# Second-layer values: four fp32 products per turn replaced by twelve split products per two turns

## The chip, the cores and the metric

One core of one Trainium2 chip runs the kernel. The metric is the device time of one execution in microseconds (us), lower is better. Engines: PE is TensorE (matmuls into PSUM), DVE is VectorE, ACT is ScalarE, POOL is GpSimd, SP issues DMAs. PSUM has eight banks of 128 x 512 fp32, PB0 to PB7.

## The reference, cut to what matters

Two layers over x of 16 x 64 rows of 512 (1024 rows), all in fp32, each an attention and a feed-forward part with residual additions. The change lies in the second layer's attention (16 query heads, 4 key heads of 96, keys and values from context and latents together: 128 positions per batch element) and in the feed-forward part behind it:

```python
x = x + L0_attention(layernorm(x), ctx)          # 32 heads of 128
x = x + L0_ffn(layernorm(x))                     # top-2 of 4 low-rank experts
# L1 attention: per batch element b, key head kv, query head h
hidden = concatenate([ctx, y], axis=1)           # y = layernorm(x)
attn = softmax(q @ k.T / sqrt(96))               # 64 queries x 128 positions
out = attn @ v                                   # "values", 96 wide
x = x + out @ Wo.T
# L1 ffn: a dense product with an effective weight
x = x + layernorm(x) @ (W + sum_e w_e A_e B_e).T + bias
```

## The kernel before, in words

Products that must keep fp32 accuracy are made in one of two ways. Plain fp32 operands: one matmul, which the trace shows as two records. Or split operands: each operand is kept as a high half of type fp32r and a low half (value less high half), and `thrice` (line 1159) makes three fp32r matmuls, high x high, high x low, low x high, into the same bank. The high half is made by an ACT copy, the low half by a DVE or POOL subtraction.

`plan()` writes one list of steps by hand, and every engine walks the same list and issues, for each step, only its own part. So the order of the list is the order of each engine's queue. `stage` and `tile` give a step a PSUM bank; `opened` is the wait until the bank's last reader is through, `read` the wait until this tile has been read, `done` the wait until PE has filled it.

The second layer's attention works in 32 turns s of four batch elements and two query heads of a key head (key head j = s // 8, quarter qd, head pair pr = s % 2). Two successive turns, 2t and 2t+1, give one pair t, and from it come two output tiles n = 2t and 2t+1. The loop over `it` (line 332, it = 1 to 32) runs a pipeline. One iteration holds, for PE in this order: `c1(it-2)` (four transposes of the probabilities into bank 3, PT), `b1(it-1)` (scores into bank 2), sometimes `v1` or `k1`, until it = 28 a quarter of a query projection `q1` (nine split products), `e1(it-5)` (the output product of one tile, nine split products), `d1(it-2)` (the values of one turn: four fp32 matmuls of 128 columns, eight records, line 1352, into bank 4 or 5), and for it = 29 to 32 `weff` (four matmuls, line 1374, for the effective dense weight).

Around them stand in the same list:
- DVE: row maximum of `b1` (line 1109); `low1(it-3)`, three subtractions of 256 elements that give the low halves of a turn's values (line 1132); `norm1` (reciprocal, line 1117, and multiplication, 1119); the residual addition of `e1` (line 945); for it = 29 to 32 `stats` (966, 968) and `weff`, which adds the product to `w1T` (1149); at it = 32 `rstd`, twelve small operations one after the other (979 to 990).
- ACT: `c1` is the move of the transposed probabilities out of bank 3 (`pTb`); `b1` four exponentials and four read-outs of their sums (913); `d1` three moves of 256 elements which make the high halves of the values `Oh`; for it = 29 to 31 `weff_split`, which waits for DVE's `weff` addition.
- POOL: low halves of weights.

Behind the loop (lines 371 to 404, "the tail") stand `c1(31)`, `weff_split(3)`, `low1(30)`, `e1(28)`, two normalisations `xn`, `d1(31)`, `low1(31)`, `e1(29)`, four transposed tiles `xT(3, 0..3)` with `e1(30)` between the second and the third, `e1(31)`, the statistics and `rstd` of the upper rows, the dense products 0 to 2, `xT` 4 and 5, dense 3, `xT` 6 and 7, dense 4 to 7. Each `e1` adds its result into 128 rows of x, and the second half of the rows can be normalised only when `e1(31)` has been added.

`PACK` (line 12) says how heads of 96 rows are laid into tiles of 128: six pieces of 96, 32, 64, 64, 96 and 32 rows.

Of the kernel before, what the change touches and what calls it, by code (L numbers as in the profile page):

```python
# [62 lines left out]
def plan():  # L63
# [268 lines left out]
    for it in range(1, N1 + 1):  # L332
        if 0 <= it - 2:
            stage("c1", it - 2, bank=3)
        stage("b1", it - 1, bank=2)
        if 0 <= it - 3:
            step("low1", it - 3)
        step("norm1", it - 1)
        for i in v1_plan.get(it, ()):
            v1(1, i)  # L340
# [8 lines left out]
        if 0 <= it - 2:  # L349
            stage("d1", it - 2, bank=4 + it % 2)  # L350
# [27 lines left out]
    stage("d1", N1 - 1, bank=5)  # L378
    step("low1", N1 - 1)
# [39 lines left out]
def program(nc, a, out):  # L419
# [18 lines left out]
    with ExitStack() as ctx:  # L438
# [46 lines left out]
        V1 = [sb(f"V1{r}", [128, 4, 1024]) for r in range(2)]  # L485
# [24 lines left out]
        PS, PT, PA = PB[2], PB[3], PB[4:6]  # L510
# [186 lines left out]
        def gpsimd_program(e):  # L697
            pool = Lane(e)
            for kind, *k in steps:
# [51 lines left out]
                elif kind == "b0":  # L751
# [26 lines left out]
        def scalar_program(e):  # L778
# [161 lines left out]
        def vector_program(e):  # L940
# [6 lines left out]
            for kind, *k in steps:  # L947
# [163 lines left out]
                elif kind == "norm1":  # L1111
# [7 lines left out]
                    e.tensor_tensor(E3, E3, rr.unsqueeze(2).broadcast_to([128, 4, 128]), ALU.mult).then_inc(s_nrm1)  # L1119
                elif kind == "low1":  # L1120
                    s, = k
                    pr, e2, os = s % 2, s % 2, (s // 2) % 2
                    n = 0
                    for m in range(3):
                        for r0, rows, h, d0 in PACK[m]:
                            if h // 2 == pr:
                                n += 1
                                src = PA[e2][d0:d0 + rows, :].rearrange("p (b n t) -> p n b t", b=4, n=2)[:, h % 2]
                                dh, dl = (O[r0:r0 + rows, os, 256 * m:256 * m + 256].rearrange("p (b t) -> p b t", b=4)
                                          for O in (Ohp, Olp))  # L1130
                                dve.wait_ge(s_ohi1, 3 * s + 3)
                                last = e.tensor_tensor(dl, src, dh.bitcast(f32), ALU.subtract)
                    last.then_inc(free[4 + e2])
# [22 lines left out]
        def tensor_program(e):  # L1156
# [14 lines left out]
            for kind, *k in steps:  # L1171
                if kind in ("k0", "q0", "v0", "e0", "sum0", "xT", "k1", "v1", "b1", "c1", "d1", "e1", "weff",
                            "dense", "mgT", "delta"):
                    b = bank_of(kind, *k)
# [168 lines left out]
                elif kind == "d1":  # L1343
                    s, = k
                    j, qd, pr = s // 8, s % 8 // 2, s % 2
                    e2 = s % 2
                    pe.wait_ge(*read("c1", s))
                    for bb in range(4):
                        bt = 4 * qd + bb
                        pe.wait_ge(*read("v1", 0, bt // 2))  # L1350
                        pe.wait_ge(*read("v1", 1, bt // 2))
                        last = e.matmul(PA[e2][0:96, bb * 128:(bb + 1) * 128],  # L1352
                                        V1[bt % 2][:, j, 128 * (bt // 2):128 * (bt // 2) + 96],
# [105 lines left out]
```

## Time and profile before

| | |
|---|---|
| median of 3 runs | 854.36 us (853.88 to 854.86) |
| profiled execution | 854.5 us |
| span of its profile | 852.7 us |
| PE busy | 839.6 us, 98% of the span |
| DVE / ACT / POOL busy | 490.3 / 353.0 / 310.7 us |

The span runs from the first to the last instruction; what the execution's own time has over it (1.8 us) lies around them. A matmul's recorded duration is longer than its share of the stream, because matmuls are pipelined: the pace is the distance between two starts. Layer one ends near 500 us, the 32 turns run from about 599 to 813 us, the tail from there to the end.

### The profile page before, as it was taken

The page shows a single profiled execution, that of the slowest core. Times are in us where ns is not written, and L with a number is a line of the kernel's source. Part 1 is how long each engine was busy: PE and PEld are TensorE (multiplying, and loading weights), DVE is VectorE, ACT ScalarE, POOL GpSimd, SP SyncE. Part 2 cuts the span into 40 slices and gives each one's busy share as a digit, 9 for nine tenths or more (in the row PEclk, how much of TensorE's full clock was granted, in tenths as well). Part 3 has the DMA queues.
Part 4 walks back from the last instruction along what each step waited for, and adds up shares of the span by engine and source line. Part 5 has one row for each costly group of instructions (what it writes and reads, how often), then busy time and mean ns, then how long its engine had stood idle before and what let it go on. Part 6 is the DMA issues. An engine that isn't in the chain of part 4 may idle for free.

```text
span 852.7 us, 12369 instructions
## 1 busy us (share of the span) xinstructions
PE 839.6 (98%) x4758; PEld 700.2 (82%) x4758; DVE 490.3 (57%) x869; ACT 353.0 (41%) x827; POOL 310.7 (36%) x239
## 2 busy tenths in 40 slices
PE   6999999999999999999999999999999999999998
PEld 5878888888888888888877788888988888888776
DVE  6856655655555655555566536465344445455783
ACT  6443123123123123123123242667776766676642
POOL 4777534634534634534536330112010210211222
PEclk9999999999999999999999999999999999999999
DMA  8112211311211311311211122101010110310002
GB/s 302 50 64 75 86 38 41 109 38 38 87 38 39 111 38 38 87 38 40 85 38 52 46 78 81 26 26 50 13 38 13 54 47 1 107 43 1 1 1 100
DMA packets 24891, 48.15 MB, mean 56 GB/s; under 512 B 3584, under 2 KB 4736, under 8 KB 24704
## 3 DMA queue, kind: packets, MB, share of 16 engines
q1 hardware_dynamic: 24400, 47.22, 18.2%
q8 instruction: 38, 0.62, 0.3%
q14 instruction: 21, 0.17, 0.1%
q10 hardware_dynamic: 432, 0.14, 0.1%
HBM read 45.12 MB, written 2.23 MB: 56 GB/s over the span
## 4 chain that ended last, share of the span: by engine, by line
PE 93%; DVE 2%; POOL 2%; ACT 1%; DMA 1%; issue 1%; SPq 0%; POOLq 0%; DVEq 0%
PE PB L1161 22%; PE PB L1163 22%; PE PB L1162 22%; PE PB L1320 8%; PE PB L1251 4%; PE PB L1335 3%; PE PB L1225 3%; PE PB L1352 3%; PE PB L1168 3%; PE PB L1235 1%; PE PB L1272 1%; DMA xs<-in_x 1%; PE PB L1374 1%; POOL qb L730 1%; ACT Eb L809 1%
## 5 line engine op out<-in xcount | busy, mean ns | idle before, releaser
L945 DVE TENSOR_TENSOR xs<-xs,PB 128x512 f32<-128x512 f32 x112 | 76.8, 686 | 120.3 <-PE PB L1163 113.1
L730 POOL TENSOR_TENSOR qb<-qb,arena 128x512 f32<-128x512 f32 x64 | 83.7, 1308 | 151.3 <-DVE arena L1023 151.3
L781 ACT ACTIVATE Oh<-PB 128x512 fp32r<-128x512 f32 (+2 forms) x160 | 69.2, 467 | 82.7 <-PE PB L1352 44.9
L1161 PE MATMUL PB<-WOh,Oh 128*128 128x512 f32 x248 | 96.6, 390 | 0.0
L1163 PE MATMUL PB<-WOh,Ol 128*128 128x512 f32 x248 | 96.5, 389 | 0.0
L1162 PE MATMUL PB<-WOl,Oh 128*128 128x512 f32 x248 | 96.5, 389 | 0.0
L1020 DVE TENSOR_TENSOR qb<-PB,ropeq 128x512 f32<-128x512 f32 x64 | 44.2, 691 | 69.4 <-PE PB L1163 68.3
L707 POOL TENSOR_TENSOR WQl<-stage,WQh 128x512 fp32r<-128x512 f32 x38 | 49.0, 1292 | 91.4 <-ACT WQh L781 90.1
L1161 PE MATMUL PB<-xTh,WQh 128*128 128x512 f32 x192 | 76.5, 399 | 0.0
L1163 PE MATMUL PB<-xTh,WQl 128*128 128x512 f32 x192 | 74.8, 390 | 0.0
L1162 PE MATMUL PB<-xTl,WQh 128*128 128x512 f32 x192 | 74.7, 389 | 0.0
L781 ACT ACTIVATE WOh<-stage 128x512 fp32r<-128x512 f32 (+1 forms) x32 | 19.4, 619 | 132.3 <-PE PB L1163 132.3
L707 POOL TENSOR_TENSOR WOl<-stage,WOh 128x512 fp32r<-128x512 f32 (+1 forms) x32 | 40.4, 1276 | 89.4 <-ACT WOh L781 63.5
L781 ACT ACTIVATE arena<-PB 128x256 f32<-128x256 f32 (+3 forms) x56 | 26.4, 473 | 80.9 <-PE PB L1163 80.5
L1046 DVE TENSOR_TENSOR Ol<-PB,Oh 128x512 fp32r<-128x512 f32 x64 | 39.7, 683 | 33.7 <-ACT Oh L781 33.6
L1163 PEld LDWEIGHTS PB<-WOh,Ol 128*128 128x128 f32 x248 | 46.5, 188 | 9.7
L1161 PEld LDWEIGHTS PB<-WOh,Oh 128*128 128x128 f32 x248 | 46.6, 188 | 9.7
L1162 PEld LDWEIGHTS PB<-WOl,Oh 128*128 128x128 f32 x248 | 46.6, 188 | 9.6
L1109 DVE TENSOR_REDUCE sm<-PB 128x4 f32<-128x512 f32 x32 | 22.1, 691 | 52.3 <-PE PB L1335 52.3
L781 ACT ACTIVATE WQh<-stage 128x512 fp32r<-128x512 f32 x38 | 23.7, 630 | 64.6 <-PE PB L1163 63.7
L913 ACT ACTIVATE Eb<-PB,sm 128x128 f32<-128x128 f32 x128 | 45.0, 365 | 6.8 <-DVE sm L1109 6.5
L1161 PEld LDWEIGHTS PB<-xTh,WQh 128*128 128x128 f32 x192 | 36.0, 188 | 12.8 <-issue 5.8
(212 smaller groups left out, 2080.5 us busy)
## 6 DMA issues: line engine op xcount, KB each, us to landing
stage<-in_wq SPq DMA_DIRECT2D x44, 256.0 KB, 2.9
stage<-in_wo SPq DMA_DIRECT2D x44, 256.0 KB, 2.6
arena<-recs SPq DMA_DIRECT2D x32, 256.0 KB, 3.9
stage<-in_wk SPq DMA_DIRECT2D x13, 256.0 KB, 2.6
arena<-in_ctxT SPq DMA_DIRECT2D x8, 256.0 KB, 4.4
stage<-in_wv SPq DMA_DIRECT2D x8, 256.0 KB, 3.8
xs<-in_x SPq DMA_DIRECT2D x8, 256.0 KB, 5.7
out<-xs SPq DMA_DIRECT2D x8, 256.0 KB, 2.0
```

The source lines that it names most:

```text
L707: e.tensor_tensor(lo, staged[:, n % 4, 0:cols], hi.bitcast(f32), ALU.subtract).then_inc(s_wlo)
L730: e.tensor_tensor(dst, dst, tmp, ALU.add).then_inc(s_radd)
L781: return e.activation(dst, src, ACT.Copy)
L913: last = e.activation(Eb[:, e2, cols], PS[:, cols], ACT.Exp, bias=mx[:, bb:bb + 1], accum_out=rs[:, bb:bb + 1])
L945: e.tensor_tensor(xs[:, i, :], xs[:, i, :], PB[b][:, :], ALU.add).then_inc(free[b])
L1020: e.tensor_tensor(dst, src, table[:, 0:1, :].broadcast_to([128, 8, 64]), ALU.mult)
L1046: e.tensor_tensor(dl, src, dh.bitcast(f32), ALU.subtract).then_inc(free[bank_of("d0", u, h, w)])
L1161: e.matmul(dst, Ah, Bh, start=(k == 0), stop=False)
L1162: e.matmul(dst, Ah, Bl, start=False, stop=False)
L1163: return e.matmul(dst, Al, Bh, start=False, stop=(k == n - 1))
L1251: last = e.matmul(PB[b][:, 256 * c:256 * c + 256], V[rows, i, c0:c0 + 128], E0[u % 2][rows, 512 * h + 256 * c:512 * h + 256 * c + 256], st ...
L1320: last = e.matmul(PB[b][:, :], W[:, m, r], H[:, c, cols], start=(n % 12 == 0), stop=(n % 12 == 11))
```

## The change

- `d1` is done once for two turns: `d1(t)`, at odd `it`, makes for each of four batch elements three fp32r matmuls of 256 columns (128 of either turn; `pTh[:, :, cols]` is two stretches of 128), twelve in all; elements 0 and 1 go to bank 4, 2 and 3 to bank 5. Output tile n needs only the bank n % 2.
- The probabilities are split: ACT's move writes the high half `pTh` (it lies over `pTb`), and a new DVE step `p_low` writes `pTl`; bank 3 comes free with `p_low`.
- The values' weights are split by POOL, one new step `v1_split` of two operations (128 x 384 elements) per pair, a pair ahead.
- ACT's high halves of the values are a step of their own, `o_move(t, bank)`, with six moves of 128 elements; DVE's `low1(t, bank, part)` is twice three subtractions of 128 elements.
- In the tail the step for `e1(30)` stands behind dense 0, and `e1(31)` behind dense 1; only dense 2 is left between `e1(31)` and `xT` 4.
- The scratch that the program reserves for DMA descriptors is made smaller (1024).

The core of it:

```diff
+        t, h = (it - 4) // 2, it % 2
+        if t >= 0 and h == 0:
+            step("o_move", t, h)
         if 0 <= it - 2:
             stage("c1", it - 2, bank=3)
+        if t >= 0 and h == 1:
+            step("o_move", t, h)
+        if 0 <= it - 2 and h == 1:
+            step("p_low", it - 2)
         stage("b1", it - 1, bank=2)
-        if 0 <= it - 3:
-            step("low1", it - 3)
+        if t >= 0:
+            step("low1", t, h, 0)
+        if t >= 0 and h == 1:
+            step("low1", t, h, 1)
+        if 0 <= it - 2 and h == 0:
+            step("p_low", it - 2)
         step("norm1", it - 1)
+        if t >= 0 and h == 0:
+            step("low1", t, h, 1)
+        if h:
+            step("v1_split", it // 2)
...
-        if 0 <= it - 2:
-            stage("d1", it - 2, bank=4 + it % 2)
+        if it % 2 and it >= 3:
+            d1(it // 2 - 1)
...
     stage("c1", N1 - 1, bank=3)
+    t = N1 // 2 - 1
+    step("o_move", t - 1, 1)
     step("weff_split", 3)
-    step("low1", N1 - 2)
+    step("p_low", N1 - 1)
+    low1(t - 1, 1)
     stage("e1", 28)
     for i in range(2):
         step("xn", 3, i)
-    stage("d1", N1 - 1, bank=5)
-    step("low1", N1 - 1)
+    d1(t)
+    step("o_move", t, 0)
+    low1(t, 0)
     step("stats", 3, 4)
...
         if i == 1:
-            stage("e1", 30)
-            step("stats", 3, 6)
+            step("o_move", t, 1)
+            low1(t, 1)
     for i in LO:
         step("add_bias", i)
+    stage("dense", 0)
+    stage("e1", 30)
+    step("stats", 3, 6)
+    stage("dense", 1)
     stage("e1", 31)
     step("stats", 3, 7)
     step("rstd", 3, 4)
-    for i in range(3):
-        stage("dense", i)
+    stage("dense", 2)
     normed(3, HI, [None, lambda: stage("dense", 3)])
...
-                elif kind == "d1":
-                    s, = k
-                    pr, e2, os = s % 2, s % 2, (s // 2) % 2
-                    act.wait_ge(*done("d1", s))
-                    if s >= 4:
-                        act.wait_ge(*done("e1", s // 2 * 2 - 3))
+                    act.wait_ge(*done(*(("d1", s // 2 - 1, 1) if s >= 2 else ("delta", 4 * s + 3))))
+                    move(pTh[:, s % 2, :], PT[:, :]).then_inc(s_phi)
+                elif kind == "o_move":
+                    t, bank = k
+                    act.wait_ge(*done("d1", t, bank))
+                    if t >= 2:
+                        act.wait_ge(*done("e1", 2 * t - 4 + bank))
                     for m in range(3):
                         for r0, n, h, d0 in PACK[m]:
-                            if h // 2 == pr:
-                                src = PA[e2][d0:d0 + n, :].rearrange("p (b n t) -> p n b t", b=4, n=2)[:, h % 2]
-                                dh = Ohp[r0:r0 + n, os, 256 * m:256 * m + 256].rearrange("p (b t) -> p b t", b=4)
-                                move(dh, src).then_inc(s_ohi1)
+                            col = 256 * m + 128 * bank
+                            dh = Ohp[r0:r0 + n, t % 2, col:col + 128].rearrange("p (b t) -> p b t", b=2)
+                            move(dh, PA[bank][d0:d0 + n, h]).then_inc(s_ohi1)
...
+                elif kind == "p_low":
+                    s, = k
+                    dve.wait_ge(s_phi, s + 1)
+                    e.tensor_tensor(pTl[:, s % 2, :], PT[:, :], pTh[:, s % 2, :].bitcast(f32), ALU.subtract).then_inc(free[3])
                 elif kind == "low1":
+                    t, bank, part = k
+                    dve.wait_ge(s_ohi1, 12 * t + 6 * bank + 6)
...
                 elif kind == "d1":
+                    t, = k
+                    pe.wait_ge(s_vlo, t + 1)
+                    pe.wait_ge(*read("c1", 2 * t))
+                    pe.wait_ge(*read("c1", 2 * t + 1))
                     for bb in range(4):
+                        b = bank_of("d1", t, bb // 2)
+                        pe.wait_ge(*opened("d1", t, bb // 2))
+                        cols = slice(128 * bb, 128 * bb + 128)
+                        dst = PB[b][0:96, 256 * (bb % 2):256 * (bb % 2) + 256].rearrange("p (r t) -> p r t", r=2)
+                        last = thrice(dst, 0, 1, V1h[:, t % 2, bb % 2, bb // 2, :], V1l[:, t % 2, bb % 2, bb // 2, :],
+                                      pTh[:, :, cols], pTl[:, :, cols])
```

## Rows read from the trace of the kernel before

**Rows 1.** The page: busy time by engine, and the chain that ended last.
```profile
PE 839.6 (98%) x4758; PEld 700.2 (82%) x4758; DVE 490.3 (57%) x869; ACT 353.0 (41%) x827; POOL 310.7 (36%) x239
PE 93%; DVE 2%; POOL 2%; ACT 1%; DMA 1%; issue 1%; SPq 0%; POOLq 0%; DVEq 0%
```

**Rows 2.** Windows: stretch, its length, busy us (count) by engine, clock, DMA.
```profile
794.63:800.60 5.97, 5.97 (x34) 4.58 (x33) 4.93 (x11) 3.87 (x13) 1.30 (x1) 1.00 0.01 3
812.53:820.66 8.13, 6.49 (x40) 5.45 (x38) 6.08 (x23) 5.20 (x10) 3.95 (x4) 1.00 0.00 0
```

**Rows 3.** Timeline of PE, first-layer values: start us, duration us, instruction.
```profile
204.44 0.28 PE L1161 MATMUL PB<-WVh,cTh 128*128 128x256 f32 x1
207.19 0.28 PE L1163 MATMUL PB<-WVh,cTl 128*128 128x256 f32 x1
```

**Rows 4.** Timeline of PE, an iteration with `q1`: its first, and the first of `e1`.
```profile
661.78 0.48 PE L1320 MATMUL PB<-xTh,WQh 128*128 128x512 f32 x1
663.93 0.39 PE L1161 MATMUL PB<-WOh,Oh 128*128 128x512 f32 x1
```

**Rows 5.** Timeline of PE, iteration 30: `c1`, `b1`, `e1`'s first, `d1`, `weff`.
```profile
794.63 0.60 PE L1168 MATMUL PB<-ident_sb,Eb 128*128 128x128 f32 x4
795.07 1.06 PE L1335 MATMUL PB<-arena,qb 96*128 96x128 f32 x8
795.88 0.47 PE L1161 MATMUL PB<-WVh,Oh 128*128 128x512 f32 x1
...
798.01 1.04 PE L1352 MATMUL PB<-pTb,V 128*96 128x128 f32 x8
798.88 1.88 PE L1374 MATMUL PB<-arena 128*128 128x512 f32 x4
```

**Rows 6.** Timeline of PE, tail: dense 0, `xT` 4 and 5, dense 4.
```profile
825.77 0.39 PE L1161 MATMUL PB<-WQh,xTh 128*128 128x512 f32 x1
...
833.94 1.03 PE L1168 MATMUL PB<-ident_sb,Eb 128*128 128x128 f32 x8
...
838.35 0.47 PE L1161 MATMUL PB<-WQh,xTh 128*128 128x512 f32 x1
```

**Rows 7.** Timeline of ACT, iteration 30: `weff_split(0)`, `c1`, first exponential, values' high halves.
```profile
795.63 0.63 ACT L781 ACTIVATE WQh<-w1T 128x512 fp32r<-128x512 f32 x1 [1.34 <-DVE w1T L1149]
796.28 0.60 ACT L781 ACTIVATE pTb<-PB 128x512 f32<-128x512 f32 x1
796.89 0.37 ACT L913 ACTIVATE Eb<-PB,sm 128x128 f32<-128x128 f32 x1
...
799.08 1.18 ACT L781 ACTIVATE Oh<-PB 96x256 fp32r<-96x256 f32 x3 [0.69 <-PE PB L1352]
```

**Rows 8.** Timeline of DVE, iteration 30, from `weff(0)`'s addition to `weff(1)`'s.
```profile
794.91 0.69 DVE L1149 TENSOR_TENSOR w1T<-w1T,PB 128x512 f32<-128x512 f32 x1
796.17 0.69 DVE L1109 TENSOR_REDUCE sm<-PB 128x4 f32<-128x512 f32 x1 [0.57 <-PE PB L1335]
796.89 1.29 DVE L1132 TENSOR_TENSOR Ol<-PB,Oh 64x256 fp32r<-64x256 f32 x3
798.43 0.18 DVE L1117 RECIPROCAL sm<-sm 128x4 f32<-128x4 f32 x1 [0.25 <-ACT Eb L913]
...
800.09 0.69 DVE L966 BATCH_NORM_STATS2 st<-xs 128x6 f32<-128x512 f32 x1
...
800.91 0.66 DVE L1149 TENSOR_TENSOR w1T<-w1T,PB 128x512 f32<-128x512 f32 x1
```

**Rows 9.** Timeline of ACT, tail: normalisation of upper rows, after `rstd`.
```profile
830.96 1.52 ACT L809 ACTIVATE Eb<-xs,lnb 128x512 f32<-128x512 f32 x2 [6.42 <-DVE lnb L990]
```

**Rows 10.** Timeline of DVE, tail: statistics behind `e1(31)`.
```profile
827.63 0.69 DVE L966 BATCH_NORM_STATS2 st<-xs 128x6 f32<-128x512 f32 x1
```

**Rows 11.** Timeline of POOL, a low half in iteration 31.
```profile
802.31 1.29 POOL L768 TENSOR_TENSOR WQl<-w1T,WQh 128x512 fp32r<-128x512 f32 x1 [4.68 <-ACT WQh L781]
```

**Rows 12.** Timeline of PE, start of the kernel.
```profile
7.30 0.63 PE L1163 MATMUL PB<-cTh,WKl 128*128 128x512 f32 x1
```

More of the change, by code:

```diff
@@ L95, in v1, with low1, d1 @@
         stage("v1", w, i)
+    def low1(t, h):
+        for part in range(2):
+            step("low1", t, h, part)
+    def d1(t):
+        for h in range(2):
+            tile("d1", t, h, bank=4 + h)
+        step("d1", t)
     def q0(u, n):
@@ L468, in program @@
         Eb = sb("Eb", [128, 2, 512])
+        with nc.sbuf_tensor("pTh", [128, 2, 512], f32r) as pTh:
+            pass
         pTb = sb("pTb", [128, 2, 512])
+        pTl = sb("pTl", [128, 2, 512], f32r)
         Oh = sb("Oh", [128, 2, 2, 512], f32r)
@@ L484, in program @@
             pass
-        V1 = [sb(f"V1{r}", [128, 4, 1024]) for r in range(2)]
+        V1w = sb("V1", [128, 2, 4, 1024])
+        V1 = [V1w[:, r, :, :] for r in range(2)]
+        V1h = sb("V1h", [128, 2, 2, 2, 96], f32r)
+        V1l = sb("V1l", [128, 2, 2, 2, 96], f32r)
         ident = sb("ident_sb", [128, 128])
@@ L509, in program @@
         PB = [ctx.enter_context(nc.psum_tensor(f"PB{i}", [128, 512], f32)) for i in range(8)]
-        PS, PT, PA = PB[2], PB[3], PB[4:6]
+        PS, PT = PB[2], PB[3]
+        PA = [PB[4 + h][:, :].rearrange("p (b h t) -> p h b t", b=2, h=4) for h in range(2)]
         mvP = PT[:, 256:272].rearrange("p (i n) -> p i n", i=8)
@@ L756, in gpsimd_program @@
                     e.tensor_tensor(E3, E3, keep[:, :].unsqueeze(1).broadcast_to([128, 16, 64]), ALU.mult).then_inc(s_msk)
+                elif kind == "v1_split":
+                    t, = k
+                    j, qd = t // 4, t % 4
+                    src = V1w[:, :, j, 256 * qd:256 * qd + 256].rearrange("p r (i d) -> p r i d", i=2)[:, :, :, 0:96]
+                    hi, lo = V1h[:, t % 2, :, :, :], V1l[:, t % 2, :, :, :]
+                    for w in range(2):
+                        pool.wait_ge(*read("v1", w, 2 * qd))
+                        pool.wait_ge(*read("v1", w, 2 * qd + 1))
+                    if t >= 2:
+                        pool.wait_ge(*done("d1", t - 2, 1))
+                    e.tensor_scalar(hi, src, 1.0, None, ALU.mult).then_inc(s_vhi)
+                    pool.wait_ge(s_vhi, t + 1)
+                    e.tensor_tensor(lo, src, hi.bitcast(f32), ALU.subtract).then_inc(s_vlo)
                 elif kind == "weff_load":
@@ L1119, in vector_program @@
                     e.tensor_tensor(E3, E3, rr.unsqueeze(2).broadcast_to([128, 4, 128]), ALU.mult).then_inc(s_nrm1)
+                elif kind == "p_low":
+                    s, = k
+                    dve.wait_ge(s_phi, s + 1)
+                    e.tensor_tensor(pTl[:, s % 2, :], PT[:, :], pTh[:, s % 2, :].bitcast(f32), ALU.subtract).then_inc(free[3])
                 elif kind == "low1":
[L1121 to L1133, printed above, removed]
+                    t, bank, part = k
+                    dve.wait_ge(s_ohi1, 12 * t + 6 * bank + 6)
+                    for m, r0, rows, h, d0 in [(m, *piece) for m in range(3) for piece in PACK[m]][3 * part:3 * part + 3]:
+                        col = 256 * m + 128 * bank
+                        dh, dl = (O[r0:r0 + rows, t % 2, col:col + 128].rearrange("p (b t) -> p b t", b=2)
+                                  for O in (Ohp, Olp))
+                        last = e.tensor_tensor(dl, PA[bank][d0:d0 + rows, h], dh.bitcast(f32), ALU.subtract)
+                    if part:
+                        last.then_inc(free[4 + bank])
                 elif kind == "e1":
@@ L1343, in tensor_program @@
                 elif kind == "d1":
[L1344 to L1347, printed above, removed]
+                    t, = k
+                    pe.wait_ge(s_vlo, t + 1)
+                    pe.wait_ge(*read("c1", 2 * t))
+                    pe.wait_ge(*read("c1", 2 * t + 1))
                     for bb in range(4):
[L1349 to L1353, printed above, removed]
-                                        pTb[:, e2, bb * 128:(bb + 1) * 128], start=True, stop=True)
-                    last.then_inc(full[b])
+                        b = bank_of("d1", t, bb // 2)
[4 more added lines that the diff above has]
+                                      pTh[:, :, cols], pTl[:, :, cols])
+                        if bb % 2:
+                            last.then_inc(full[b])
                 elif kind == "e1":
@@ L1359, in tensor_program @@
                     qd, c = i // 2, i % 2
[L1360 to L1363 removed]
+                    t = 4 * j + qd
+                    os = t % 2
+                    pe.wait_ge(*read("d1", t, c))
                     for m in range(3):
```

12 lines of the change are left out of this document (4 added, 8 removed).

## The prediction

> **What bounds the kernel now.** I read the page first, then windows by iteration, then the timelines of PE, ACT and DVE in one iteration. The page shows PE busy for 98% and on the ending chain for 93%, with DVE at 57% and ACT at 41% [rows 1]. So PE time removed is time gained, as long as the others stay hidden. The window of one late iteration says how much room they have: in 5.97 us DVE is busy for 4.93 and ACT for 3.87, against the page's shares; from c1(31) to e1(30), 8.13 us long, PE is busy for only 6.49 [rows 2]: there it already waits 1.64 us for DVE. The change moves work from PE to ACT and DVE, and the late iterations and the tail are where that can cost.
>
> **PE's saving.** The new product has 256 columns in fp32r, as the first layer's values: 24 of them start between 204.44 and 207.19, 23 gaps of 0.120 us [rows 3]. Twelve take 1.44 us. For the rest of an iteration, `q1` takes 663.93 - 661.78 = 2.15 us [rows 4]; `c1` 0.44, `b1` 0.81, `e1` 2.13, an old `d1` 0.87, `weff` 1.71 [rows 5], and the whole 5.97 [rows 2]. Behind `q1`, without the switch from fp32, `e1` takes nine times the pace of the dense products, 36 of which fill 825.77 to 833.94, 0.227 each [rows 6]: 2.04. Two old `d1` are 1.74 us, so a pair saves 0.30, and 13 pairs (iterations 3 to 28) save 4.0 us. Bounds: nothing lies below half the 512-column pace (0.113, twelve are 1.36: 0.38 a pair) and the upper end is that two stretches of 128 don't stream as one of 256 (a rival below).
> The Trainium skill, "TensorE: Matmul & The Clock Gate", section Back-to-back issue gap, would put a 256-column matmul at 262 cycles, 0.109 us. By that a pair takes 1.31 us and 13 pairs save 5.6. The row has 0.120 for the same shape, and the row decides.
>
> **Prices on the other engines.** ACT moves 512 elements in 0.60 and three times 256 in 1.18 us, 0.39 each [rows 7]: 0.29 for 128 by the line through both. Six (`o_move`) are 1.7 us an iteration, before 1.18. Lower end: four exponentials and four read-outs take 1.54 from 796.89 to the reciprocal at 798.43 [rows 7, 8], 0.19 each, six are 1.2; upper end the 256 price, six are 2.4. DVE: 256 elements 0.43, 512 0.69 [rows 8], by the same line 0.29 for 128; six (`low1`) are 1.75, before 1.29; ends 0.18 (the four-element reciprocal) and 0.43, so 1.1 to 2.6. `p_low` has the size and type of the additions out of PSUM, 0.69, one more per iteration (0.62 to 0.69 when queued). I take the line, since both neighbours are of the same operation. The others: maximum starts 1.53 after `c1`'s start, exponentials 0.72 after the maximum, reciprocal 1.54 after them, `norm1` 0.9 in all, addition 0.7, statistics 0.9, `weff` addition 0.66, `weff_split` 0.65 [rows 5, 7, 8].
>
> **Iterations 3 to 28: hidden.** Without `d1` an even iteration lasts 0.44 + 0.81 + 2.15 + 2.04 = 5.44, an odd one 6.88. Even, from `c1`'s start: o_move 0.2 to 1.9, `pTh` to 2.5, exponentials from 2.4, reciprocal 3.9, norm1 done 4.8; the next `c1` comes at 5.44. DVE fits `low1`'s first half (2.2 to 3.05) and `p_low` (to 3.7) into the wait. Odd: `pTh` to 1.25, o_move to 2.85, `p_low` to 1.95, maximum to 2.6, exponentials to 4.3, `low1` 2.9 to 4.65, norm1 done 5.5, next `c1` 6.88. Bank 5 is asked for by `d1` at 5.44 + 0.72 = 6.2 and is free at 4.65. With `v1` or `k1` iterations are longer. So nothing waits, and this cover is PE's `q1`.
>
> **Iterations 29 to 32: a loop appears.** `q1` is gone, and the list is: `weff` addition (DVE), `weff_split` (ACT), then, behind it in ACT's queue, `o_move`, `pTh` and exponentials; behind those in DVE's queue `low1`, `norm1`, the addition, the statistics, and the next `weff` addition. Each engine waits for the other. From `c1`'s start in each:
> - 29: `wo1`'s split delays ACT to 0.9; pTh 1.5, o_move 3.1, low1 3.15 to 4.9; d1's second half, wanted at 4.1, starts 4.95; weff ends 7.4. Length 7.4.
> - 30: weff addition to 0.97, weff_split 1.6, o_move 3.3, pTh 3.9, exponentials from 3.8, reciprocal 5.35, norm1 6.25: `c1` at 6.35 where PE is through at 5.1. DVE goes on with low1 7.1, addition 7.8, statistics 8.7, weff addition 9.45. Length 6.35.
> - 31: so weff_split only at 3.1 to 3.8; pTh 4.3, o_move 5.9, p_low 5.0, maximum 5.65, low1 5.9 to 7.7. d1 (wanted at 3.4) starts 5.1, its second half 7.8, weff ends 10.2. Length 10.2.
> - 32: as 30, `c1(31)` at 6.35.
> Together 30.3 against 4 x 5.97 = 23.9: 6.4 lost, the saving of their `d1` included.
>
> **The tail.** From `c1(31)` = 0: DVE finishes low1 at 0.8, addition 1.5, statistics 2.4, `rstd` 4.9 (12 operations, about 2.4: 827.63 to 830.96 with the statistics, 3.33 [rows 9, 10]), weff addition 5.6; only behind these come p_low(31), done 6.3, and low1(14,1), done 8.0. Before, `d1(31)` needed neither of DVE. e1(28) ends at 2.9, `d1` starts at 6.4, its second half at 8.1, ends 8.8. e1(29) to 10.9, xT 0 and 1 to 11.7; xn(2) and xn(3) wait for these, xT 2 and 3 end 14.1; dense 0 from 14.4, e1(30), dense 1, e1(31) to 23.9 (dense 2.72 each: 825.77 to 833.94 are three [rows 6]), dense 2 to 26.6. Addition, statistics, rstd and the first xn behind e1(31) take 0.3 + 0.7 + 3.33 + 0.8 = 5.1: xT 4 starts at 29.1, 2.5 late, with xn(5) 0.35 more. Before it started 833.94 - 812.53 = 21.4 after `c1(31)`. So 8.0 lost. The 1.64 wait goes, but 3.5 + 1.0 before `d1`, 1.7 at xT 2 and 3, and 2.5 at xT 4 take its place. From dense 4 all is as before.
>
> **Sum.** -4.0 + 6.4 + 8.0 = +10.4 us. The profiled execution took 854.5 (span 852.7), 0.1 over the median of the runs: **864.9 us**. With the small pieces at the low ends the loop shrinks by about 1 us an iteration, +6; at the upper ends by as much longer, +15. POOL's two new operations of 384 elements are at most 1.29 each [rows 11] in a pair of 12 us, needed an iteration later: nothing. The smaller scratch: nothing, since PE waits for no DMA; what cover is lost if a load came late isn't seen.
>
> **Rivals.**
> - *The loop doesn't close, PE stays the bound* (other side): from one `weff` addition to the next I have about 8 us; it decides at 5.8, the mean PE work of iterations 29 to 32. For it: 1.0 us of DVE is idle in such an iteration and ACT has 2.1 [rows 2]. Then 16 x 0.30 and the 1.64 are gained, and only xT 4's 2.85 and about 0.5 of xT 2 are paid: 854.5 - 3.1 = 851.4, faster. Against: the serial order of the list. Chance 0.14.
> - *Small pieces near their low ends*: same mechanism, 860.5. It is in my own range.
> - *The clock falls in the long wait before `d1(15)`*: at the start of the kernel a 512-column product takes 0.63 us [rows 12] against 0.39 [rows 4], 0.24 more, which is about 512 columns at 1.2 instead of 2.4 GHz. The 1.64 us wait of before passed at a granted clock of 1.00 [rows 2]; nothing shows one of 3.5. If it is enough, e1(29)'s nine products cost 0.24 each more: 867. Chance 0.10. The Trainium skill, same page, section HAM oscillation — how this bites in real kernels, says that idle gaps between bursts bring the half rate back; by that rule the time would be this one.
> - *Two stretches of 128 run in four passes*: twelve at 0.427 are 5.1 us, 16 x (5.1 - 1.74) = +54 on top of nothing, about 909. `b1` and `c1` with fp32 are such; the operand type speaks against. Chance 0.01.
>
> **Chances and range.** My forecast with its own range (859 to 869.5) 0.70; clock 0.10; loop open 0.14; partly open (854 to 859) 0.05; passes 0.01. 0.2% (1.7 us) is about what can be told from no change: faster 0.13, same 0.05, slower 0.82. The range 856 to 869.5 leaves out the open loop and a little above.
>
> **What would show it.** Right: `d1` as 12 records of 256 columns at 0.120; PE without gaps to iteration 28; PE waits before `c1(29)`, in `d1(14)` and before `d1(15)` for DVE's `p_low` and `low1`, xT 4 waiting for xn. Wrong: an iteration 31 below 7 us, `d1(15)` within 1 us of e1(28)'s end, or gaps in iterations 5 to 28, which would mean that the small pieces cost more than the line says.

## The result and the profile after

| | before | after |
|---|---|---|
| median | 854.30 us (4 runs, 853.88 to 854.86) | 868.66 us (4 runs, 866.61 to 869.57) |
| ratio | | 1.0164 [1.0148, 1.0180] |
| profiled execution, its span | 854.5, 852.7 us | 868.5, 866.7 us |

The change makes the kernel 1.6% slower. The prediction, 864.9 us, had the direction; the result is 3.8 us above it and inside the range. (The first column has one run more than the median given ahead of the prediction, so 854.30 stands for 854.36.)

The page of the changed kernel answers to [rows 1]:
```profile
PE 841.4 (97%) x4694; PEld 696.9 (80%) x4694; DVE 525.3 (61%) x997; ACT 370.3 (43%) x923; POOL 346.6 (40%) x271
PE 90%; DVE 3%; ACT 3%; POOL 2%; issue 1%; DMA 1%; SPq 0%; POOLq 0%; DVEq 0%; ACTq 0%
```
PE has 64 records fewer and yet is recorded busy 1.8 us longer, although the new products are cheaper: other work of PE must have become dearer, and the windows below show which. DVE gained 35.0 us, ACT 17.3, POOL 35.9, and the ending chain goes through DVE and ACT for 6% instead of 3%.

PE's waits from 780 us on (total, times, longest). Before, this list had one line, 1.6 us for DVE's `Ol`:
```profile
PE PB L1213 <- DVE pTl L1175: 4.4, 2, 2.9
PE PB L1220 <- ACT Eb L863: 3.5, 3, 2.3
PE PB L1213 <- DVE Ol L1183: 3.5, 4, 1.7
PE PB L1220 <- DVE Eb L1171: 1.6, 2, 1.1
```
That is 13.0 us of waiting. PE's timeline shows where it lies. First the steady part (the new product's first and last record, then the start of `c1(27)`), then iterations 30 to 32 and the tail:
```profile
617.05 0.28 PE L1213 MATMUL PB<-pTh,V1h 128*96 128x256 f32 x1
...
618.35 0.28 PE L1215 MATMUL PB<-pTh,V1l 128*96 128x256 f32 x1
618.47 0.60 PE L1220 MATMUL PB<-ident_sb,Eb 128*128 128x128 f32 x4
...
784.58 0.60 PE L1220 MATMUL PB<-ident_sb,Eb 128*128 128x128 f32 x4
...
789.61 0.36 PE L1213 MATMUL PB<-pTh,V1h 128*96 128x256 f32 x1 [0.75 <-DVE Ol L1183]
...
798.48 0.63 PE L1220 MATMUL PB<-ident_sb,Eb 128*128 128x128 f32 x4 [1.08 <-DVE Eb L1171]
...
803.51 0.33 PE L1213 MATMUL PB<-pTh,V1h 128*96 128x256 f32 x1 [1.46 <-DVE pTl L1175]
...
806.15 0.53 PE L1213 MATMUL PB<-pTh,V1h 128*96 128x256 f32 x1 [1.73 <-DVE Ol L1183]
...
807.55 3.62 PE L1426 MATMUL PB<-arena 128*128 128x512 f32 x4
...
817.29 0.63 PE L1220 MATMUL PB<-ident_sb,Eb 128*128 128x128 f32 x4 [0.56 <-DVE Eb L1171]
...
823.45 0.33 PE L1213 MATMUL PB<-pTh,V1h 128*96 128x256 f32 x1 [2.93 <-DVE pTl L1175]
...
847.60 1.36 PE L1220 MATMUL PB<-ident_sb,Eb 128*128 128x128 f32 x8 [2.30 <-ACT Eb L863]
```
Twelve products take 618.47 - 617.05 = 1.42 us, and up to iteration 28 PE waits only once, in iteration 5 (below). The second half of `d1(13)` waits 0.75 (789.61). Then `d1(14)` (803.51, its second half 806.15) and `d1(15)` (823.45) wait for the low halves that DVE must now make, and `xT` 4 (847.60) for a normalisation. The `weff` product at 807.55 is recorded with 3.62 us where the one of [rows 5] had 1.88. (Its four records are two fp32 matmuls of 512 columns, two records each, not four matmuls as said ahead of the prediction. The transposes of `c1`, one record each, are the exception to two records for a plain fp32 product.) Windows say why (the third column from the right is PE's granted clock):
```profile
806.15:811.50 5.35, 5.35 (x13) 3.18 (x14) 2.71 (x6) 0.00 (x0) 0.00 (x0) 0.50 0.00 0
825.60:828.60 3.00, 3.00 (x11) 2.43 (x10) 2.03 (x8) 0.88 (x4) 1.67 (x2) 0.50 0.00 0
845.00:849.00 4.00, 1.65 (x11) 1.11 (x10) 2.02 (x10) 2.23 (x3) 1.38 (x2) 1.00 0.17 66
```
Behind the waits of `d1(14)` and of `d1(15)` PE ran at 0.50, the lower of its two levels (1.2 GHz). Behind `xT` 4's wait of 2.30 us (third window) and behind [rows 2]'s of 1.64 it did not. This is most of the 3.8 us that the prediction lacks.

DVE and ACT in iteration 31, answering to [rows 7, 8], show the loop of queues. DVE first:
```profile
800.84 0.66 DVE L1201 TENSOR_TENSOR w1T<-w1T,PB 128x512 f32<-128x512 f32 x1
802.67 0.69 DVE L1175 TENSOR_TENSOR pTl<-PB,pTh 128x512 fp32r<-128x512 f32 x1 [1.18 <-ACT pTh L835]
...
804.30 1.79 DVE L1183 TENSOR_TENSOR Ol<-PB,Oh 96x128 fp32r<-96x128 f32 x6 [0.34 <-ACT Oh L835]
```
and ACT beside it:
```profile
801.52 0.63 ACT L835 ACTIVATE WQh<-w1T 128x512 fp32r<-128x512 f32 x1 [4.13 <-DVE w1T L1201]
802.06 0.58 ACT L835 ACTIVATE pTh<-PB 128x512 fp32r<-128x512 f32 x1
802.54 1.73 ACT L835 ACTIVATE Oh<-PB 96x128 fp32r<-96x128 f32 x6
```
ACT stood idle for 4.13 us because the first instruction in its queue, the split of an effective weight, waited for DVE's addition to `w1T`. The moves of `pTh` and `Oh`, whose inputs were long there, stood behind it. DVE waits for them with `p_low` and `low1`, and its own queue carries the next addition behind those.

### The profile page after: what moved, and what is told of

Its sections match the earlier page's. It is cut to its first block, busy times and chain, and to the rows that moved or that the text cites. A ratio compares the mean times of both kernels' runs of the same rounds, so it can differ in the third digit from the quotient of the medians.

```text
span 866.7 us, 12534 instructions
## 1 busy us (share of the span) xinstructions
PE 841.4 (97%) x4694; PEld 696.9 (80%) x4694; DVE 525.3 (61%) x997; ACT 370.3 (43%) x923; POOL 346.6 (40%) x271
## 4 chain that ended last, share of the span: by engine, by line
PE 90%; DVE 3%; ACT 3%; POOL 2%; issue 1%; DMA 1%; SPq 0%; POOLq 0%; DVEq 0%; ACTq 0%
PE PB L1213 23%; PE PB L1215 22%; PE PB L1214 22%; PE PB L1372 8%; PE PB L1303 4%; PE PB L1277 3%; PE PB L1387 3%; PE PB L1220 3%; PE PB L1287 1%; PE PB L1324 1%; DVE Ol L1183 1%; ACT Eb L863 1%; ACT Oh L835 1%; DMA xs<-in_x 1%; POOL qb L771 1%
## 5 line engine op out<-in xcount | busy, mean ns | idle before, releaser
L835 ACT ACTIVATE Oh<-PB 32x128 fp32r<-32x128 f32 (+3 forms) x256 | 84.8, 353 | 54.8 <-PE PB L1303 36.8
L1183 DVE TENSOR_TENSOR Ol<-PB,Oh 96x128 fp32r<-96x128 f32 (+1 forms) x192 | 55.0, 286 | 10.7 <-ACT Oh L835 8.3
```

Source lines behind the costliest of these rows:

```text
L835: return e.activation(dst, src, ACT.Copy)
L1183: last = e.tensor_tensor(dl, PA[bank][d0:d0 + rows, h], dh.bitcast(f32), ALU.subtract)
```

## The experiments

Ten kernels ran, each beside the kernel before, in batches (e1 to e4; e5 to e8; e9 and e10) whose medians of the kernel before are 854.46, 854.41 and 854.48 us. Diffs are against the changed kernel unless another is named. Gains and losses are differences of medians; the ratio to the kernel before stands beside each.

**e1: the loop cut open.** One line moves the split of each effective weight one iteration later, when DVE's addition has long been made.
```diff
-        if N1 - 4 < it < N1:
-            step("weff_split", it - 29)
+        if N1 - 3 < it:
+            step("weff_split", it - 30)
```


> Only edit: weff_split(m) stands one iteration later (30, 31, 32 instead of 29, 30, 31), so that ACT finds weff's addition done when it comes to it. Theory (iterations 29 to 32 are slow because DVE's weff addition, ACT's weff_split, o_move, low1 and norm1 form a closed loop over both queues): c1(29) and c1(31) come when PE is through (iterations 30 and 32 about 5.1 us instead of 6.3), iteration 31 falls from 12.5 to about 8.5 with the clock staying up, p_low(31) comes 0.6 earlier; together about 7 us: 861.5. Rival (DVE simply has more work than PE in these iterations, the loop through ACT is not what counts): iterations 29 to 32 stay within 1.5 us of the 32.7 us they take now, time 867 to 869.

Measured: 862.34 us (861.32 to 862.73), ratio to before 1.009 [1.0076, 1.0104]; 6.3 us less than the changed kernel. PE's timeline, the last starts of `c1` and the waits between them and in the tail:
```profile
791.97 0.60 PE L1220 MATMUL PB<-ident_sb,Eb 128*128 128x128 f32 x4
797.11 0.60 PE L1220 MATMUL PB<-ident_sb,Eb 128*128 128x128 f32 x4
802.77 0.36 PE L1213 MATMUL PB<-pTh,V1h 128*96 128x256 f32 x1 [1.29 <-DVE Ol L1183]
805.28 0.60 PE L1220 MATMUL PB<-ident_sb,Eb 128*128 128x128 f32 x4
810.39 0.60 PE L1220 MATMUL PB<-ident_sb,Eb 128*128 128x128 f32 x4
...
816.29 0.33 PE L1213 MATMUL PB<-pTh,V1h 128*96 128x256 f32 x1 [2.92 <-DVE pTl L1175]
```
Iterations 30, 31, 32 last 5.14, 8.17, 5.11 us. The even ones are bound by PE again, as the list alone said; `d1(14)` keeps one wait, `d1(15)` its whole 2.92. From `c1(27)` to `c1(31)` it is 26.0 us instead of 32.7, and the rival of this run had no more than 1.5 us of change there. The loop is shown, and so is that it isn't the whole loss. But not all of the 6.3 us is the queues' own: with the first of `d1(14)`'s two waits gone, the clock stayed at 1.00 in iteration 31 too. e8 below runs the same stretch with the loop closed and the clock up in 30.3 us, so that of the 6.8 us between the two profiles there 4.4 are the loop's and 2.4 the clock's.

**e2: `rstd` behind `low1(14)`.** The twelve small DVE operations stand ahead of `p_low(31)`; here they are moved behind what `d1(15)` needs.
```diff
-        if it == N1:
-            step("rstd", 3, 0)
...
     low1(t - 1, 1)
+    step("rstd", 3, 0)
     stage("e1", 28)
```


> Only edit: rstd(3, 0), twelve small DVE operations of 2.3 us together, stands behind p_low(31) and low1(14, 1) instead of ahead of them. Theory (d1(15) waits because p_low(31) and low1(14, 1) are queued behind rstd on DVE): d1(15) starts 2.3 us earlier, its wait falls from 2.9 to about 0.6, the clock does not fall in e1(29), which gives 1.4 more; xn(0) and xn(1) come later but not after e1(29): about 3.5 us less, 865. Rival (the rows' normalisation is as late as before, so the wait only moves to xT 0): within 0.7 us of the changed kernel.

Measured: 872.13 us (871.36 to 872.52), 1.0205 [1.0191, 1.0219]: slower than the changed kernel by 3.5. The expected gain was there and was given back. PE's timeline:
```profile
819.84 0.33 PE L1212 MATMUL PB<-pTh,V1h 128*96 128x256 f32 x1 [0.53 <-DVE pTl L1174]
...
828.08 0.63 PE L1219 MATMUL PB<-ident_sb,Eb 128*128 128x128 f32 x4 [1.98 <-ACT Eb L862]
...
832.21 0.76 PE L1212 MATMUL PB<-WQh,xTh 128*128 128x512 f32 x1 [1.71 <-issue]
```
and the window of its dense 0:
```profile
832.21:836.10 3.89, 3.89 (x9) 3.10 (x10) 3.41 (x9) 0.28 (x1) 0.00 (x0) 0.50 0.00 0
```
`d1(15)` waits 0.53 instead of 2.93. But the first `xn` starts only at 823.81, when `rstd` is through, ACT's `o_move(15, 0)` stands between the first two and the last two `xn`, and `low1(15, 0)` comes at 827.13. `xT` 2 then waits 1.98, dense 0 starts 1.71 us after PE went idle, and dense 0 runs at 0.50. The DVE queue held two urgent things, and turning them round chose which is late. PE's waits from 780 us on add up to 14.5 us instead of 13.0; that is only part of the loss. The rest goes with the clock, which here also fell behind `xT` 4's wait: the mean granted clock of the four runs is 0.990 to 0.992, where the changed kernel's runs have 0.994 to 0.996.

**e3: the tail's order as before.** The dense tiles go back behind the outputs; the product of 256 columns stays.
```diff
             low1(t, 1)
+            stage("e1", 30)
+            step("stats", 3, 6)
     for i in LO:
         step("add_bias", i)
-    stage("dense", 0)
-    stage("e1", 30)
-    step("stats", 3, 6)
-    stage("dense", 1)
     stage("e1", 31)
...
-    stage("dense", 2)
+    for i in range(3):
+        stage("dense", i)
```


> Only edit: e1(30) again between xT 1 and xT 2, e1(31) ahead of dense 0, dense 0 to 2 behind it (the order of the kernel before). Theory (the new order costs the 2.3 us wait of xT 4, because only dense 2 covers the chain addition, statistics, rstd, xn; but it also covers low1(15, 1)): the wait at xT 4 goes, e1(30) covers the waits of xT 2 and 3 (1.25 us), and e1(31) waits about 3 us for low1(15, 1): about 1.3 us less, 867.4. Rival (dense ahead of e1 is a gain by itself, as it fills the old 1.64 us wait): slower than the changed kernel by 1 to 2 us.

Measured: 867.63 us (864.12 to 869.82, 5 runs), 1.0154 [1.0131, 1.0178]. The interval holds the changed kernel's ratio, so the second part of the change neither gained nor lost anything that shows. The median is near what was expected (867.4), 1.0 us less than the changed kernel, but the two intervals together allow 2.4 us either way: they decide neither for that nor against the low end of the rival. In PE's timeline the wait of `e1(31)`'s first product takes the place of `xT` 4's, which is what the reordering traded:
```profile
835.04 0.50 PE L1212 MATMUL PB<-WVh,Oh 128*128 128x512 f32 x1 [2.79 <-DVE Ol L1182]
```
A window of iteration 31:
```profile
806.15:811.50 5.35, 5.33 (x29) 4.06 (x30) 3.81 (x7) 1.79 (x6) 1.19 (x1) 1.00 0.00 0
```
This is the window of the same 5.35 us as in the changed kernel, with the same list up to there and the same wait of 1.73 before it. This time the clock stayed at 1.00. It fell further back, behind `d1(15)`'s wait of 2.93 us and behind the 2.79 above:
```profile
823.00:829.00 6.00, 6.00 (x22) 5.02 (x22) 3.76 (x11) 1.22 (x6) 1.95 (x2) 0.53 0.00 0
835.04:839.00 3.96, 3.96 (x10) 3.12 (x11) 2.71 (x5) 0.00 (x0) 0.00 (x0) 0.57 0.00 0
```
The spread of these runs, 5.7 us, is wider than that of the other kernels, and it goes with the mean granted clock of each run: 864.12 us at 0.998, 867.63 at 0.996, 867.56 at 0.994, 869.82 at 0.992, 869.23 at 0.990.

**e4: PE kept busy in the waits.** Twenty-five products of the identity with itself are added: 6 before `d1(14)`, 7 before its second half, 12 before `d1(15)`. They write banks that are free and are overwritten, and nothing reads them.
```diff
+                    if t >= 14:
+                        b = bank_of("d1", t, 0)
+                        pe.wait_ge(*opened("d1", t, 0))
+                        for _ in range({14: 6, 15: 12}[t]):
+                            e.matmul(PB[b][:, 0:128], ident[:, :], ident[:, :], start=True, stop=True)
                     pe.wait_ge(s_vlo, t + 1)
```
(and the same seven times ahead of `d1(14)`'s third batch element, in the bank of `weff(2)`)

> Only edit: 25 fp32 products of the identity by itself (0.21 us each), whose results are overwritten, stand in the waits: 6 ahead of d1(14), 7 ahead of its second half, 12 ahead of d1(15). Nothing that is computed changes. Theory (PE's idle time ahead of d1(14)'s second half and d1(15) lets its clock fall to 0.50, and weff(2), c1(30) and e1(29) then run at half pace): granted clock 1.00 there, weff(2) takes 1.7 instead of 3.4 us, e1(29) 2.1 instead of 3.5; about 4.2 us less, 864.3. Rival (the clock falls for another reason, such as what the other engines do): no gain, 868 to 869.

Measured: 866.59 us (864.75 to 866.83), 1.0137 [1.0123, 1.0151]: 2.1 less than the changed kernel, where 4 were expected. Windows at the first filled wait and behind `xT` 4's unfilled one:
```profile
802.00:808.90 6.90, 6.63 (x45) 5.23 (x44) 5.45 (x13) 3.86 (x16) 3.42 (x3) 1.00 0.01 2
845.00:849.00 4.00, 3.95 (x13) 3.19 (x14) 1.38 (x2) 2.48 (x4) 4.00 (x4) 0.62 0.15 57
```
Where the waits are filled the clock holds, so the rival, a cause in the other engines, is out. It fell instead behind the wait that I had left, where the changed kernel's profile has 1.00 in the same stretch. One of the four runs had a mean clock of 1.000 and took 864.75 us; the other three, at 0.998, took 866.45 to 866.83. So this one fall costs about 1.9 us.

**e8: the fourth wait filled too.** Against e4, ten such products more ahead of `xT` 4.
```diff
+                    if ph == 3 and i == 4:
+                        for _ in range(10):
+                            e.matmul(PB[b][:, 0:128], ident[:, :], ident[:, :], start=True, stop=True)
                     pe.wait_ge(*xn_done(ph, i))
```


> e4_fill (866.6) with ten more products of the identity (2.1 us) in the wait of xT 4, which passed at clock 1.00 in the changed kernel but was followed by 0.50 in e4_fill. Nothing that is computed changes. Theory (a fall of the clock follows a long wait, now here, now there): no stretch behind iteration 28 at a clock below 1.00; 1.5 us less than e4_fill, 865, and 3.6 less than the changed kernel, which is then the whole price of the clock. Rival (the fall belongs to the place): no change against e4_fill.

Measured: 865.11 us (864.83 to 866.09), 1.0127 [1.0113, 1.0141]. All four runs have a mean granted clock of 1.000, and the windows have 1.00 throughout:
```profile
785.00:815.00 30.00, 26.89 (x149) 20.22 (x148) 22.06 (x51) 16.47 (x64) 9.42 (x8) 1.00 0.00 1
815.00:845.00 30.00, 27.18 (x154) 22.58 (x155) 23.03 (x69) 12.69 (x31) 7.21 (x6) 1.00 0.06 23
845.00:863.00 18.00, 14.99 (x72) 12.20 (x70) 6.11 (x9) 3.36 (x6) 4.13 (x4) 1.00 0.21 81
```
The whole price of the clock is 868.66 - 865.11 = 3.55 us by the medians, 3.5 by the two spans (866.7 and 863.2), and 3.2 by the two ratios, give or take 1.8 by their intervals. The added products delay nothing that shows: `d1(15)` starts 6.16 us after `c1(31)` in both profiles. Without the clock's falls the changed kernel stands at 865.1, where the prediction had 864.9.

**e5: the new product where it has cover.** Pairs 0 to 12 as in the change; turns 26 to 31, iterations from 29 on and the tail as before.
```diff
-        if it % 2 and it >= 3:
+        if it % 2 and 3 <= it <= 27:
             d1(it // 2 - 1)
+        if it >= 28:
+            stage("dx", it - 2, bank=4 + it % 2)
...
-        if 0 <= it - 2 and h == 1:
+        if 0 <= it - 2 < 26 and h == 1:
             step("p_low", it - 2)
```
(`dx` is the four fp32 products of a turn of before, `lowx` its low halves; for t = 12 both banks' moves and low halves stand in iteration 28)

> Edit: pairs 0 to 12 (turns 0 to 25) as in the changed kernel, turns 26 to 31 as in the kernel before (four fp32 products each, three moves and three subtractions of 256 elements, bank 3 freed by ACT's move), and from iteration 29 on the order and the tail of the kernel before. Theory (the products themselves gain 0.30 us a pair; all the loss comes from iterations 29 to 32 and the tail, where PE no longer covers the added ACT and DVE work): 13 x 0.30 gained, 0.9 paid in iteration 5 where b1(4) waits for ACT's k1 move: 851.4, 3.0 less than the kernel before. Rival (the added work of ACT, DVE and POOL also costs in iterations 5 to 28, or the profile's stretch of iterations 6 to 28 says too much): 854 or more.

Measured: 853.11 us (852.68 to 854.27, 11 runs), 0.9986 [0.9977, 0.9995]. The first part of the change is worth something where PE has `q1` beside it, but 1.7 less than expected. (The smaller scratch is in this kernel too, as in all ten; it was never tried by itself.) PE's timeline at the change-over:
```profile
786.35 1.11 PE L1435 MATMUL PB<-pTb,V 128*96 128x128 f32 x8 [1.32 <-DVE Ol L1217]
```
Turn 26's product waits for bank 4, which pair 12 holds with both its halves' low parts in one iteration.

**e9: the change-over mended.** Against e5, pair 12's second `o_move` stands behind the exponentials, and its low halves are spread round `norm1`.
```diff
-            if t == 12:
-                step("o_move", t, 1)
...
+        if t == 12:
+            step("low1", t, 0, 1)
+            step("o_move", t, 1)
         step("norm1", it - 1)
-        if t >= 0 and h == 0:
+        if 12 > t >= 0 and h == 0:
             step("low1", t, h, 1)
...
+        if t == 12:
+            low1(t, 1)
```


> e5_hybrid with the change-over in iteration 28 mended: o_move(12, 1) behind the exponentials instead of ahead of them, the second half of low1(12, 0) ahead of norm1. Theory (e5_hybrid missed 851.4 by 1.7 only because its turn 26 waited 1.32 us for bank 4, whose reader was queued behind twelve moves on ACT): that wait goes, 851.8. Rival (something else in it): 853.

Measured: 851.67 us (851.31 to 851.81), 0.9964 [0.9952, 0.9977]: faster than both kernels. PE's waits from 595 us on are two, the old one before `e1(29)` and one in iteration 5:
```profile
PE PB L1248 <- DVE Ol L1209: 1.7, 1, 1.7
PE PB L1422 <- ACT arena L841: 0.9, 1, 0.9
```

**e6 and e10: the wait in iteration 5.** In the changed kernel `b1(4)` waits 0.94 us at 626.15 for ACT's move of keys made just before. e6 is e5 with that group of keys an iteration earlier (`k1_plan = {3: (0, 1, 1), ...` for `{4: (0, 1, 1), ...`):

> e5_hybrid with one more edit: k1(0, 1, 1) in iteration 3 instead of 4, so that its move out of PSUM is an iteration older when b1(4) reads it. Theory (b1(4)'s wait of 0.94 us is for this move, which came later against b1 because even iterations have lost their d1): the wait and 0.2 of switching go, 0.9 to 1.1 less than e5_hybrid, 850.4. Rival (the move only delays another wait): as e5_hybrid.

Measured: 856.13 us (854.81 to 857.34, 11 runs), 1.0016 [1.0007, 1.0025], slower than e5 by 3.0. In the profile the wait went, and a longer one came:
```profile
627.48 0.63 PE L1254 MATMUL PB<-ident_sb,Eb 128*128 128x128 f32 x4 [1.92 <-DVE Eb L1194]
```
The product it holds up is `c1(3)`. In ACT's timeline of iteration 4 the keys' two moves end at 621.96; behind them stand a weight split (0.63), the six moves of `o_move` (1.74) and the move of `pTh` (0.60), so the exponentials start only at 624.90 and DVE's normalisation ends at 627.33. But the profiled run took 854.84, 1.4 above e5's profiled run; the rest of the 3.0 goes with the clock. The five runs at a mean clock of 0.999 or 1.000 took 854.81 to 855.60 us, the six at 0.997 or 0.998 took 856.13 to 857.34. Where it fell in those six no profile shows.

e10 is e9 with the group ahead of `q1` in its own iteration:
```diff
+        if it == 4:
+            k1(*k1_plan.pop(it))
         if it <= 28:
```


> e9_hybrid2 with one more edit: in iteration 4 the product k1(0, 1, 1) stands ahead of q1 instead of behind it, 2.1 us earlier, in the same iteration (in iteration 3 it blocked ACT's queue and cost 3 us). Theory: ACT's move of it is over before b1(4) asks, its wait of 0.94 us goes and with it the late exponentials: 850.9, 3.5 less than the kernel before. Rival (q1's moves are now late in its place): 852 or more.

Measured: 851.62 us (851.16 to 851.84), 0.9964 [0.9950, 0.9977]: no difference from e9. The same product waits 0.89. The view names no releaser, but in ACT's timeline the move of the queries now comes behind that of the keys and ends at 626.13, just before the product starts:
```profile
626.23 1.13 PE L1424 MATMUL PB<-arena,qb 96*128 96x128 f32 x8 [0.89 <-issue]
...
622.89 1.20 ACT L843 ACTIVATE arena<-PB 96x512 f32<-96x512 f32 x2 [0.54 <-PE PB L1252]
624.94 1.19 ACT L965 ACTIVATE qb<-PB 96x512 f32<-96x512 f32 x2 [0.84 <-PE PB L1409]
```
The cover that iteration 5 lost is the old `d1(2)` between the keys' product and `b1(4)`.

**e7: the last pair together.** Against e1, with the tail's order of before, and the second half of the last pair moved and split right behind the first.
```diff
     low1(t, 0)
+    step("o_move", t, 1)
+    low1(t, 1)
     step("stats", 3, 4)
```


> e1_split_later (862.3) with another tail: e1(30) and e1(31) where the kernel before has them, and o_move(15, 1) and low1(15, 1) directly behind o_move(15, 0) and low1(15, 0). Theory (the waits in the tail behind e1(29) are all caused by the place of o_move(15, 1) and by the two dense products ahead of e1(31)): the waits of xT 2, xT 3, dense 0 and xT 4 go (0.56 + 0.69 + 0.3 + 2.3 us), e1(30) and e1(31) don't wait; 4 us less, 858.3; the wait of 2.9 us ahead of d1(15) stays. Rival (what is taken from one wait appears in another, as with rstd moved later): 861 or more.

Measured: 857.29 us (856.93 to 858.91), 1.0038 [1.0026, 1.0051], 5.0 below e1. Two kinds of wait are left from 780 us on:
```profile
PE PB L1212 <- DVE pTl L1174: 2.9, 1, 2.9
PE PB L1212 <- DVE Ol L1182: 2.0, 2, 1.3
```
With its steps in a better order the kernel is still 2.9 us slower than the one before: what the first 28 iterations gain is less than what iterations 29 to 32 and the tail lose. Part of that is the clock, 0.58 from 817.45 to 821.50 us behind the 2.9 us wait; the five runs have 0.996 to 0.998.

## Why the prediction came out as it did

The two profiled executions, cut at the starts of `c1`:

| stretch | before | after | difference | predicted |
|---|---|---|---|---|
| start to `c1(27)` | 788.64 | 784.58 | -4.1 | -4.0 |
| iteration 29 | 5.99 | 7.54 | +1.5 | +1.4 |
| iteration 30 | 5.97 | 6.36 | +0.4 | +0.4 |
| iteration 31 | 5.97 | 12.48 | +6.5 | +4.2 |
| iteration 32 | 5.96 | 6.33 | +0.4 | +0.4 |
| `c1(31)` to `xT` 4 | 21.41 | 30.31 | +8.9 | +7.7 |
| `xT` 4 to the end | 18.76 | 19.10 | +0.3 | +0.3 |
| sum | 852.7 | 866.7 | +14.0 | +10.4 |

- **PE's saving: right, by two errors that cancel.** The pace is 0.118 us a product, near the 0.120 read from [rows 3]. But I counted 26 old products against 13 new ones, and by iteration 28 there were 27 of the old (27 x 0.87 = 23.5 against 13 x 1.42 = 18.5, 5.0 saved). The wait of `b1(4)`, 0.94, which I hadn't foreseen ("So nothing waits"), took the surplus. That the number came out right is luck (and 13 x 0.30 is 3.9, not 4.0). e9, which makes turn 26 in iteration 28 as before, is 3.4 us ahead of the kernel before at `c1(27)`; 13 x 0.32 less the wait is 3.2. I had looked at ACT's load in an ordinary iteration, not in one with `k1`, which I took to be longer and so safe: it was longer, but its move stands at its end. A gap in iterations 5 to 28 was my own sign that the small pieces cost more than the line says; the gap came, and not for that reason.
- **Small prices: right.** Grouped by line over 600 to 830 us (count | busy us, mean ns | idle before): DVE's `p_low` and `low1`, ACT's `o_move`, POOL's `v1_split`:
```profile
L1175 DVE TENSOR_TENSOR pTl<-PB,pTh 128x512 fp32r<-128x512 f32 x32 | 21.8, 682 | 12.5 <-ACT pTh L835 12.5
L1183 DVE TENSOR_TENSOR Ol<-PB,Oh 96x128 fp32r<-96x128 f32 x62 | 17.7, 285 | 7.8 <-ACT Oh L835 7.4
L835 ACT ACTIVATE Oh<-PB 96x128 fp32r<-96x128 f32 x62 | 16.8, 271 | 14.8 <-PE PB L1215 14.0
L808 POOL TENSOR_SCALAR V1h<-V 128x384 fp32r<-128x384 f32 x15 | 17.6, 1172 | 17.4 <-PE PB L1215 17.4
L810 POOL TENSOR_TENSOR V1l<-V,V1h 128x384 fp32r<-128x384 f32 x15 | 15.3, 1017 | 1.3
```
  The line through the 256 and 512 element prices gave 0.29 for both; they are 0.285 and 0.271, which answers the rival of pieces near their low ends (860.5). POOL's two are under the 1.29 bound and nobody waits for them.
- **The loop: right,** iteration by iteration, and e1 confirms its cause. With the clock up (e8) the four iterations take 30.3 us, as forecast (30.3). The open-loop rival (851.4) is out.
- **The tail: right.** Predicted waits before `d1(15)` of 3.5 and 1.0 were 2.93 and 0.70; those of `xT` 2 and 3, 1.7 together, were 0.56 and 0.69, `xT` 4's 2.5 was 2.30. With the clock up (e8) `xT` 4 starts 29.2 us after `c1(31)`; the forecast had 29.1.
- **What failed: the clock.** I had it as a rival, at one place, the wait before `d1(15)`, at +2.1 and a chance of 0.10, because [rows 2]'s 1.64 us wait passed at 1.00. It fell at two places. In iteration 31 the excess over the prediction is 2.3: the second half of `d1(14)` (1.40 instead of about 0.70) and `weff` (3.41 instead of 1.72 to the next start) ran at half pace. The next `c1` did too, but that only shortened the wait behind it (0.56, where e8 has 1.02). In the tail it is 1.2: `e1(29)` takes 829.49 - 826.01 = 3.48 instead of 2.13. Together 3.5, and e8 measures 3.55 without any of it. The rival should have been read from all the waits that my own working had listed: two in `d1(14)` of 1.7 and 2.0 near each other (they measured 1.46 and 1.73), 3.5 ahead of `d1(15)` (2.93), 2.5 at `xT` 4 (2.30). I priced only the longest. Of the two times on record, the rival's 867 came nearer than the 864.9.
  The Trainium skill, "TensorE: Matmul & The Clock Gate", section HAM oscillation — how this bites in real kernels, says that idle gaps between bursts of matmuls bring the half rate back. The runs agree that it happens and that filling the gaps prevents it (e8: 1.00 throughout). It is regular only for the longest of them, as PE's waits behind 595 us in all the profiles show:

| PE's wait | clock fell during it or soon behind it | stayed at 1.00 |
|---|---|---|
| 2.79 to 2.93 us | changed kernel, e1, e3 (twice), e7 | |
| 2.30 (`xT` 4) | e2, e4 | changed kernel, e1 |
| 1.46 and 1.73, 0.9 apart | changed kernel, e2 | e3 |
| 1.98 and 0.69 (`xT` 2 and 3) | e2 | |
| one of 1.29 to 1.92 | | before, e1, e5, e6, e7, e9, e10 |

- **The second part of the change** (dense tiles ahead of the last outputs) I had costed inside the tail and never by itself; e3 puts it at no measurable difference.
- **The rival of four passes** (909) is out: the new products start 0.118 us apart. Its remark counted `c1` with `b1`; but four transposes of `c1` take 0.44 and four products of `b1` 0.81 [rows 5], so `c1` has half of `b1`'s price.

The runs that weren't profiled tell something too, for each has its mean granted clock. All four of the changed kernel have 0.994 to 0.996, so the falls belong to it and weren't chance of the profiled run; the kernel before, e5, e9 and e10 have 0.999 or 1.000 in every run, and e8 1.000. What stays open is in which place it falls in a given run, and why the middle rows of the table go either way.

## What to carry to other kernels

A cheaper product on the bounding engine is worth its saving only in those iterations in which the engines that prepare it have cover; where an iteration is short, keep the old form (e9: the same product in 13 pairs of 16 gives -2.8 us beside the batch's 854.5, in all 16, with the tail's new order, it gives +14.4). In a list that every engine walks in order, look for a pair of steps in which each engine's queue head waits for the other; e1 got 6.3 us back with one step an iteration later (about two thirds of it the loop's, one third the clock's), while moving a step into a queue that is itself late (e2, e6) only moved the wait and lost 3.5 and 3.0 us, part of it by the clock. Read the mean granted clock of every run before two medians are compared: in e3, e4 and e6 it tells the shorter runs from the longer. When a forecast contains several new waits of PE, give each of them the clock's price as well.

## What the runs showed of the hardware

- PE's granted clock fell to 0.50 behind each of five waits of 2.79 to 2.93 us, behind two of four of 2.30, and at waits of 1.46 and 1.73 us that were 0.9 us apart in two of three profiles; behind 1.64 in the kernel before it did not. At the lower level two fp32 matmuls of 512 columns took 3.41 us instead of 1.72, and `c1` 0.85 instead of 0.44.
- The granted clock of the profile doesn't show the start of the kernel: PE, idle for its first 4.06 us and again for 1.58 before 6.30, starts products of 512 columns 0.43 us apart up to 9.86 us and 0.23 apart from 10.17 us on, and the clock reads 1.00 in both stretches.
- 35 products of 128 columns of the identity, put into the four waits, kept it at 1.00 and were worth 3.55 us (e8). With one wait of 2.3 us unfilled (e4) the clock fell there (0.62 over 4 us), where it had not in the changed kernel's profile; e4's run without a fall was about 1.9 us shorter than its other three.
- fp32r products of two separate stretches of 128 columns keep the pace of 256 columns in one piece: 0.118 us against 0.120 [rows 3], a weight load with each.
